# Moving the low half of the attention context from VectorE to GpSimd

## What is computed

```
qkv = (xn @ qkv_w.T).reshape(B, S, 3, H, D)          # H = 16 heads, D = 64, S = 512
q, k = rope(q, c, s), rope(k, c, s)                  # rotation by position
scores = einsum('bhqd,bhkd->bhqk', q, k) / 8
kb = -p * log1p(a * |i - j|)                         # a bias by distance, per head
attn = softmax(scores + kb)
out = einsum('bhqk,bhkd->bhqd', attn, v)             # the context
return out.transpose(0, 2, 1, 3).reshape(B, S, H * D) @ out_w.T
```

## Time and profile before

| | |
|---|---|
| median of 3 runs | 1342.48 us (1341.34 to 1347.08) |
| the profiled execution | 1339.31 us, of it the span of the core 1337.5 |
| TensorE matmul busy | 1216.2 us, 91% of the span |
| VectorE busy | 1098.9 us, 82% |
| ScalarE busy | 985.9 us, 74% |
| GpSimd busy | 798.0 us, 60% |
| mean granted TensorE clock | 0.968 |

### The profile page before, as it was taken

The page is one execution under the profiler, slowest core; times in us unless marked ns, Lnnn a source line. Parts: engine busy times, 40 slices in busy tenths (PEclk is TensorE's granted clock), DMA queues, the critical chain, the costliest instruction groups (busy, mean ns, idle before and its releaser), DMA issues.

```text
span 1337.5 us, 33943 instructions
## 1 busy us (share of the span) xinstructions
PE 1216.2 (91%) x13412; PEld 938.0 (70%) x13412; DVE 1098.9 (82%) x2166; ACT 985.9 (74%) x1831; POOL 798.0 (60%) x628
## 2 busy tenths in 40 slices
PE   5630999997699999999999999999999999999995
PEld 5620788895267777777777777777777777777764
DVE  7864799994388888888888888888888888888894
ACT  2775688882388777777778777877778777877773
POOL 3044000001788887886788788877778887886600
PEclk9975899998899999999999999999999999999998
DMA  8625666661445444444553454355445444444411
GB/s 267 237 62 187 219 236 234 234 212 40 117 123 141 104 111 127 120 117 115 147 154 98 112 151 104 96 141 142 117 130 146 105 112 127 120 118 113 135 41 48
DMA packets 172685, 182.47 MB, mean 136 GB/s; under 512 B 78066, under 2 KB 150783, under 8 KB 172528
## 3 DMA queue, kind: packets, MB, share of 16 engines
q1 hardware_dynamic: 160256, 160.03, 41.9%
q0 software_dynamic: 4352, 12.41, 2.7%
q10 hardware_dynamic: 7920, 7.87, 2.0%
HBM read 109.12 MB, written 54.56 MB: 122 GB/s over the span
## 4 chain that ended last, share of the span: by engine, by line
PE 71%; ACT 1%; DMA 1%; issue 1%; DVE 1%; SPq 0%; ACTq 0%; DVEq 0%
PE ps_t L1307 17%; PE ps_o L1323 13%; PE ps_x L1263 13%; PE ps_s L1296 8%; PE ps_s L1297 8%; PE ps_x L1283 7%; PE ps_x L1273 6%; ACT prob L1111 1%; DMA kswap<-qk_dram 0%; DMA qk_dram<-parts 0%; DMA ot<-ctx_parts 0%; ACT proj L1073 0%; ACT prob L1073 0%; DVE ctx_parts L1193 0%; ACT pt_hi L1087 0%
## 5 line engine op out<-in xcount | busy, mean ns | idle before, releaser
L1172 DVE SCALAR_TENSOR_TENSOR pt_lo<-ps_t,pt_hi 128x1024 f16<-128x1024 f32 x256 | 312.6, 1221 | 129.1 <-ACT pt_hi L1087 129.1
L1207 DVE CUSTOM_DVE_ANT_0 neg<-ps_s,strips,score_scale 128x512 f32<-128x512 f32 x512 | 361.7, 743 | 8.1 <-PE ps_s L1297 8.0
L1111 ACT ACTIVATE prob<-neg,neg_max 128x512 f32<-128x512 f32 x512 | 362.6, 712 | 0.0
L1087 ACT ACTIVATE pt_hi<-ps_t 128x1024 f16<-128x1024 f32 x256 | 261.9, 1023 | 128.5 <-PE ps_t L1307 126.5
L1307 PE MATMUL ps_t<-ident,prob 128*128 128x128 f32 x2048 | 269.4, 273 | 4.3 <-ACT prob L1111 4.2
L1307 PEld LDWEIGHTS ps_t<-ident,prob 128*128 128x128 f32 x2048 | 234.3, 141 | 39.1 <-issue 10.6
L1323 PE MATMUL ps_o<-val_hi,pt_hi 128*128 128x64 f16 x2048 | 206.0, 193 | 1.8 <-DVE pt_lo L1172 1.7
L1323 PE MATMUL ps_o<-val_hi,pt_lo 128*128 128x64 f16 x2048 | 206.2, 193 | 0.0
L1323 PE MATMUL ps_o<-val_lo,pt_hi 128*128 128x64 f16 x2048 | 206.2, 193 | 0.0
L1296 PE MATMUL ps_s<-qk 128*128 128x512 f16 x512 | 195.4, 382 | 6.0 <-DMA kswap<-qk_dram 5.6
L1297 PE MATMUL ps_s<-kswap,qk 128*128 128x512 f16 x512 | 194.9, 381 | 0.0
(11 more groups left out here) (186 smaller groups left out, 2565.0 us busy)
## 6 DMA issues: line engine op xcount, KB each, us to landing
raw<-in_L_ffn_w_dram SPq DMA_DIRECT2D x32, 1024.0 KB, 5.1
qk_dram<-parts SPq DMA_DIRECT2D x128, 256.0 KB
qk<-qk_dram SPq DMA_DIRECT2D x32, 1024.0 KB, 5.6
kswap<-qk_dram SPq DMA_DIRECT2D x64, 256.0 KB, 6.5
xa<-in_L_attn_x_dram SPq DMA_DIRECT2D x8, 512.0 KB, 6.4
xt_dram<-xth SPq DMA_DIRECT2D x8, 512.0 KB, 5.1
slots_dram<-zeros SPq DMA_DIRECT2D x4, 1024.0 KB, 8.3
xa<-slots_dram SPq DMA_DIRECT2D x16, 256.0 KB, 5.3
```

Source lines behind the costliest of these rows:

```text
L1087: nc.scalar.activation(pt[0][:, (l - 1) % 2].rearrange("p q k c -> p q (k c)"), ps_t[l % 2][:], ACT.Copy, scale=P_SCALE).then_inc(turned_h ...
L1111: nc.scalar.activation(prob[:, l % 2, q, :], neg[:, l % 2, q, :], ACT.Exp, bias=neg_max[:, 2 * (l % 2) + q:2 * (l % 2) + q + 1], scale=-1. ...
L1172: nc.vector.scalar_tensor_tensor(out=pt[1][:, (l - 1) % 2].rearrange("p q k c -> p q (k c)"), in0=ps_t[l % 2][:], scalar=P_SCALE, in1=pt[0 ...
L1207: nc.vector.tensor_tensor_reduce(neg[:, l % 2, q, :], ps_s[q][:], strips[:, h, start:start + S], score_scale[:, 0:1], 3.0e38, ALU.add, ALU ...
```

## The change

The low half of the context is made by GpSimd (`context_low`): of the odd unit between the two rotations of a step, of the even unit behind the step and its gathers; the last unit's behind everything. The factor 1 / P_SCALE, which the two split instructions applied, goes into the reciprocal: a `tensor_scalar` multiplies `sums` by P_SCALE ahead of it, so `ctxt` is the context itself; ScalarE's high part becomes a plain copy. Before `ctxt` is written, VectorE now waits until GpSimd has made the low half of the unit before.

```diff
+            def context_low(unit):
+                pool.wait_ge(ctx_hi, unit + 1)
+                nc.gpsimd.tensor_tensor(ctx_parts[:, 1, unit % 2], ctxt[:], ctx_parts[:, 0, unit % 2], ALU.subtract).then_inc(ctx_lo, 1)
-            def step(F, fills):
+            def step(F, fills, unit=-1):
                 for w in range(2):
+                    if w and unit >= 0:
+                        context_low(unit)
                     rotate(F, w, fills + 2 * w + 2)
...
-                        step(2 * n + r, fills_before(b, 8 * j))
+                        step(2 * n + r, fills_before(b, 8 * j), 2 * (4 * b + j) - 1)
+                    else:
+                        context_low(2 * (4 * b + j) - 1)
                     if is_first(b) and j == 0:
                         combine(0, 1)
                     if not is_last(b) and j:
...
+                    context_low(2 * (4 * b + j))
...
             over_batches(batch)
+            context_low(8 * NB - 1)
...
-                nc.scalar.activation(ctx_parts[:, 0, two], ctxt[:], ACT.Copy, scale=1.0 / P_SCALE).then_inc(ctx_hi, 1)
+                nc.scalar.copy(ctx_parts[:, 0, two], ctxt[:]).then_inc(ctx_hi, 1)
...
-                nc.vector.reciprocal(rsum[:], sums[:, two, :]).then_inc(chain, 1)
-                dve.wait_ge(chain, unit + 1)
+                nc.vector.tensor_scalar(rsum[:], sums[:, two, :], P_SCALE, None, ALU.mult).then_inc(chain, 1)
+                dve.wait_ge(chain, 2 * unit + 1)
+                nc.vector.reciprocal(rsum[:], rsum[:]).then_inc(chain, 1)
+                dve.wait_ge(chain, 2 * unit + 2)
+                wait(dve, ctx_lo, unit)
                 nc.vector.tensor_tensor(ctxt[:].rearrange("p t (h d) -> p h t d", h=2),
...
-            def context_lo(b, l):
...
-                dve.wait_ge(ctx_hi, unit + 1)
-                nc.vector.scalar_tensor_tensor(out=ctx_parts[:, 1, two], in0=ctxt[:], scalar=1.0 / P_SCALE, in1=ctx_parts[:, 0, two],
-                                               op0=ALU.mult, op1=ALU.subtract).then_inc(ctx_lo, 1)
...
-                if l % 4 == 3 and not (is_first(b) and l == 3):
-                    context_lo(b, l - 1)
...
-            context_lo(NB - 1, PAIRS + 2)
```

More of the change, by code:

```diff
@@ L1186, in read_context @@
                                         ALU.mult).then_inc(ctx_read, 1)
-            def context_lo(b, l):
-                unit = PAIRS // 4 * b + (l - 6) // 4
-                two = (l - 6) // 4 % 2
-                dve.wait_ge(ctx_hi, unit + 1)
-                nc.vector.scalar_tensor_tensor(out=ctx_parts[:, 1, two], in0=ctxt[:], scalar=1.0 / P_SCALE, in1=ctx_parts[:, 0, two],
-                                               op0=ALU.mult, op1=ALU.subtract).then_inc(ctx_lo, 1)
             def slot(b, l):
```

## The result

| | before | after |
|---|---|---|
| median | 1336.26 us (17 runs, 1333.92 to 1347.08) | 1349.97 us (17 runs, 1342.41 to 1356.96) |
| profiled execution, span in it | 1339.31, 1337.5 us | 1353.46, 1351.7 us |
| TensorE / VectorE / GpSimd busy | 91% / 82% / 60% | 91% / 79% / 64% |
| mean granted clock | 0.968 | 0.939 |

The ratio of the mean times is 1.0088, with an interval from 1.0063 to 1.0113: slower, by more than the 0.5% that can be told from no change. Forecast were 1351 us and an increase of 9.0 us. The ratio says 11.8 us of the 1336.26, the two medians 13.7, the two profiled executions 14.2; the steady part, as shown next, says less than forecast. Runs of either kernel fall into two groups 7 to 9 us apart (before 11 runs around 1335.8 us and 6 around 1344.5, after 6 around 1346.6 and 11 around 1353.5).

A forecast was written before the change was run, and what follows sets the result against it. TensorE, busy at full clock in steady attention, was taken as the bound. Terms -2.3 - 0.4 + 9.0 + 1.7 + 0.7 + 0.3 = +9.0 us on the 1342.48 median gave 1351 us; range 1343 to 1409, own range 1346 to 1357.

The forecast's parts named there:

- The bound: Steady attention: TensorE always busy at clock 1.00, so time changes only where a matmul starts later or sooner.
- the ceiling: Most that relief of VectorE can bring in steady groups: 0.13 us of 30.08, about 4 us in 30 groups.
- What went from VectorE: Low half leaves slots 3 and 7: slot 5 regains 0.08 us, 2.3 us in all, plus 0.4 in batch 0.
- What came: VectorE's context reads, slots 2 and 6: 0.23 us more chain before neg, costing 29 x (0.08 + 0.23) = 9.0 us.
- The second wait: VectorE's added wait for ctx_lo before the context read: 0.03 us, otherwise free.
- Sum per group: Steady group of eight slots: 0.08 us lost in slot 3, 0.23 in slot 7, 0.08 regained in slot 5.
- The subtraction of 128x512: GpSimd's 64 new low-half subtractions: 1.16 us each, between 1.07 and 1.27, fitting into GpSimd's idle time.
- the forecast place: GpSimd's cast to the high half moves by 0.61 us, from 803.09 to 803.70, after 0.33 of rotation stretch goes.
- The gap: Slot 6: tensor_scalar at 804.78 starts just before GpSimd's subtraction at 804.82; rival that it loses: +57 us, chance 0.27.
- The first group: Batch 0's first context read: tensor_scalar waits for GpSimd's running subtraction, about 1.7 us, once; it lasts 1.9.
- The end: Last low half on GpSimd at 1.16 us for 0.70, plus 0.23 of chain: 0.7 us; last two groups 0.3.
- The total: Whole kernel: +9.0 us on the profiled 1339.31 and on the median 1342.48, giving 1351 us.

The follow-up runs named there:

- The last kernel: Changed kernel with the factor applied by ScalarE, reciprocal one slot earlier, last unit's low half back on VectorE: 1333.97 us, ratio 0.9949 to the kernel before.
- the small instruction alone: Kernel before with only the tensor_scalar added ahead of the reciprocal and ScalarE's plain copy, low half still on VectorE: 1390.14 us, ratio 1.0335.
- another order: Changed kernel with GpSimd's two casts in front of its two subtractions: 1370.58 us, ratio 1.0203.
- more reciprocals: Changed kernel with the reciprocal taken three times instead of once in each context read: 1426.76 us (one run).
- the repeat: Changed kernel without any edit, measured again in a later session beside the kernel before: 1354.88 us against 1340.72, ratio 1.0069.
- earlier by a slot: Changed kernel with tensor_scalar and reciprocal moved from slots 2 and 6 to slots 1 and 5, ahead of pt_lo: 1343.86 us, ratio 0.9991 to before.
- two small ones: Changed kernel with two tensor_scalar by 128 in place of the one by P_SCALE: 1441.87 us (one run).

## Why the prediction was right

- **The bound.** TensorE at full clock, with 0.13 us per group lost to VectorE and little more to gain: right in kind. The last kernel gained 0.17 a group, 5 us in 29, so the ceiling was set a little low.
- **What went from VectorE.** Slot 5's step fell to 0.21 us (0.22 forecast), the wait for `val_lo` vanished.
- **What came.** `tensor_scalar` to reciprocal is 0.20 us (800.80 to 801.00 in slot 2), as forecast. The second wait was put at 0.03 and costs nothing: reciprocal to read is 0.24 (816.02 to 816.26) against 0.23 in before, but it is 0.24 too in the kernel with the small instruction alone, which hasn't got this wait, and the reciprocal itself takes 202 ns there and in the change against 191 in before. So the chain grew by 0.21. In slot 3 this gave 0.05 for 0.08, in slot 7 a step of 0.43 for "about 0.50", with 0.04 more on the tile before it: 0.20, nearly the whole chain, as the prediction had it. Sum per group 0.19 for 0.23; over the 28 groups from the second read to the 58th, 842.2 to 847.6 us.
- **GpSimd.** The subtraction of 128x512 takes 1.163 us in the mean, forecast 1.16:

```profile
L1017 POOL TENSOR_TENSOR ctx_parts<-ctxt,ctx_parts 128x512 f16<-128x512 f32 x64 | 74.4, 1163 | 56.8 <-ACT ctx_parts L1108 56.5
```

  The Trainium skill, "GPSIMD Engine Reference", section "Instruction dispatch", gives the floor from which 1.07 us was estimated; the measurement is 9% above it, as a floor allows. The rotation's stretched addition is gone too (mean of line 1002: 1355 ns before, 1284 after), so the cast came at the forecast place.
- **The gap.** The forecast put cast's end, `tensor_scalar` and subtraction at 804.74, 804.78 and 804.82. In the trace they are at 815.83, 815.83 and 815.91 of a later group. It held in all steady groups. How thin the margin is, the kernels with another order and with more reciprocals show. The Trainium skill, "SBUF — State Buffer", section "Who interferes with whom", says that the holder of the port pair keeps it for a whole instruction and the other blocks. The traces agree where GpSimd is the holder: in seven profiled executions 238 of these `tensor_scalar` took over 0.25 us, and each ended within 0.03 us of the end of a GpSimd instruction that was running when it started.
- **The first group.** 1.92 us for the `tensor_scalar`, 1.9 forecast. What the sum left out is the clock behind it: TensorE was idle for 1.99 us and then ran about 3 us at the lower level. From first score to first reciprocal it is +1.6 (26.8 for 25.2), from there to the reciprocal of the next unit +0.7 more: 2.3 where 1.7 - 0.4 = 1.3 was forecast. From the 58th read to the last it is +0.7, where about 0.5 was forecast (a last steady group's 0.23 and the 0.3).
- **The end.** From the first small instruction of the last read to the transposing DMA it is 2.39 us before and 3.09 after, the forecast's 0.7. The chain that ended last, of before (beside the earlier trace rows) and of after (there from a row of VectorE's timeline on):

```profile
1321.03 0.21 DVE rsum L1181
...
1323.42 3.66 DMA ot<-ctx_parts
...
1330.72 2.75 PE ps_x L1283 x12
```
```profile
1335.84 0.17 DVE L1192 TENSOR_SCALAR rsum<-sums 128x8 f32<-128x8 f32 x1 [0.97 <-PE ps_o L1326]
...
1338.93 3.62 DMA ot<-ctx_parts
...
1346.18 1.50 PE ps_x L1286 x12
```

  From the last reciprocal on, the end as a whole was 0.8 shorter, since the second half of the last projection took 1.50 us there, at clock 1.00, and 2.75 in before, at 0.50. In the repeat it took 2.75 again, at 0.50, and the end was 0.5 longer than before's. Of the +7.6 in all, then, about 1.3 us are a gain of this one execution.
- **The total.** From the first scores on it is +7.6 us, and +8.5 in the repeat, where +9.0 stood: mechanism and size were right. That the median came out at 1349.97, so near to 1351, is luck. The base was 1342.48 from three runs and 1336.26 from seventeen, and the medians' difference of 13.7 is larger than the forecast's, as more runs of the change than of before (11 of 17 against 6) were in the longer group. The term missing in the sum and in the range's reasoning is the stretch before the scores, about 10 us either way, in code that nothing touched.

## What to carry to other kernels

The length of an instruction said little here; what stood behind it on its engine decided. 0.2 us in front of the score reader cost 0.19 us a group, while up to 1.28 us one slot earlier left the group at before's length (30.09 and 30.08). And on VectorE, before adding even the smallest `tensor_scalar`, look at what GpSimd runs at that moment in every group, and at how a few tenths of delay elsewhere would move it; where another engine can take the small operation, that risk goes. Lastly, set one stretch against another in two traces before believing a difference of medians under 1%.

## What the hardware showed beyond that

- VectorE's 128x8 f32 `tensor_scalar` takes 0.16 us, or up to 1.92 when it starts inside an arithmetic instruction of GpSimd, of one input or two. It still took 0.16 us where GpSimd's instruction had about 0.1 us left, and in the two cases of the kernel "earlier by a slot" where it started within 0.01 us of GpSimd's start. The 128x8 f32 reciprocal was never held: 150 of 150 took 202 to 204 ns in the run with three of them, all beginning and ending inside one of GpSimd's instructions.
- Where TensorE was idle for 1.97 us or more at the first context read (the change and its repeat, the small instruction alone, two small ones, more reciprocals), its clock was at 0.50 for about 3 us soon behind it. In the other five profiled executions, which have no such wait there, it stayed at 1.00.
- At the start of attention, in the same code, the granted clock was at 0.50 for 3 to 7 us in six profiled executions before it rose, and for 37 to 44 us in four. It moves a run of 1340 us by about 10.
